# A two-layer recurrent network on one core: three gating products moved from GpSimd to VectorE

## The reference

```python
xc = silu(conv(x_in)); p = xc @ W_x
delta = softplus(p[..., :D_STATE] @ W_dt + b_dt)
h = h * d_t[:, None, :] + B_t[:, :, None] * x_t[:, None, :]   # scan over t
ys = h.sum(axis=1) * C_t
y = ys * silu(res); s = y @ W_out
...
gate = zeros_like(probs).at[arange, topk_i].add(topk_p)        # top 4 of 16
act = gelu(xt @ routed_up) * gate
g = shared + act @ routed_down
x = x + s * silu(g)
```

## Time and profile before

| | |
|---|---|
| median of 3 runs | 760.62 us (760.37 to 761.76) |
| the profiled execution | 760.88 us |
| its span, first to last instruction | 759.1 us |
| busy: TensorE / VectorE / ScalarE / GpSimd | 649.5 / 671.9 / 506.1 / 339.0 us |
| mean granted TensorE clock | 0.975 of full speed |

### The profile page before, as it was taken

One profiled execution on the slowest core, in us unless ns is written; L12 is line 12 of the kernel. 1 busy time (PEld: TensorE's weight loads), 2 busy tenths in 40 slices (PEclk: granted clock), 3 DMA queues, 4 the chain that ended last, 5 costly groups with the idle time before them and its releaser, 6 DMA issues. The chain is left out here.

```text
span 759.1 us, 10868 instructions
## 1 busy us (share of the span) xinstructions
PE 649.5 (86%) x2711; PEld 300.9 (40%) x2711; DVE 671.9 (89%) x1435; ACT 506.1 (67%) x800; POOL 339.0 (45%) x310
## 2 busy tenths in 40 slices
PE   3795999999999975679989989988988988998985
PEld 1342444444444433234434434433433433443432
DVE  4996999999999997498999899898999999999885
ACT  2472566666766653786776777678678678677774
POOL 6446567776777640134224323423423423432341
PEclk9898999999999998799999999999999999999998
DMA  6430000000000000000000000000000000000000
GB/s 156 109 85 14 0 0 0 0 0 0 0 0 0 1 0 1 0 2 0 15 14 1 14 14 0 15 14 0 14 14 14 0 14 14 0 14 14 0 15 28
DMA packets 10740, 11.29 MB, mean 15 GB/s; under 512 B 4800, under 2 KB 6288, under 8 KB 10720
## 3 DMA queue, kind: packets, MB, share of 16 engines
q1 hardware_dynamic: 9744, 10.73, 4.9%
q0 software_dynamic: 112, 0.33, 0.2%
q10 hardware_dynamic: 864, 0.00, 0.1%
HBM read 6.87 MB, written 4.19 MB: 15 GB/s over the span
## 5 line engine op out<-in xcount | busy, mean ns | idle before, releaser
L1057 PE MATMUL bank<-arena,w 128*128 128x512 f16 x640 | 153.9, 389 | 20.2 <-DVE arena L723 14.1
L1057 PE MATMUL bank<-arena,dnT 128*128 128x512 f32 x288 | 145.1, 604 | 23.4 <-DVE arena L944 23.4
L618 ACT ACTIVATE arena<-bank,xinv 128x512 f32<-128x512 f32 x144 | 95.0, 687 | 58.9 <-PE bank L1057 58.8
L1057 PEld LDWEIGHTS bank<-arena,w 128*128 128x128 f16 x640 | 63.4, 100 | 99.2 <-issue 24.6
L441 POOL TENSOR_TENSOR arena<-arena 128x512 f32<-128x512 f32 x48 | 61.1, 1303 | 59.9 <-ACT arena L555 59.9
L451 POOL TENSOR_TENSOR arena<-arena 128x512 f32<-128x512 f32 x32 | 50.1, 1565 | 84.3 <-DVE arena L985 73.8
L431 POOL TENSOR_TENSOR arena<-arena 128x512 f32<-128x512 f32 x16 | 17.5, 1092 | 150.1 <-DVE arena L923 150.1
L1057 PE MATMUL bank<-xh,upH 128*128 128x512 f16 x144 | 55.9, 388 | 29.3 <-ACT arena L618 26.5
L481 ACT ACTIVATE arena<-bank 128x512 f16<-128x512 f32 x96 | 53.9, 606 | 35.0 <-PE bank L1057 35.0
L1057 PEld LDWEIGHTS bank<-arena,dnT 128*128 128x128 f32 x288 | 51.1, 190 | 62.9 <-DVE arena L944 46.4
L944 DVE TENSOR_TENSOR arena<-arena 128x512 f32<-128x512 f32 x80 | 75.8, 965 | 0.0
(11 more groups left out here) (188 smaller groups left out, 1480.2 us busy)
## 6 DMA issues: line engine op xcount, KB each, us to landing
x_all<-in_L_attn_x SPq DMA_DIRECT2D x16, 256.0 KB, 2.7
out<-x_all SPq DMA_DIRECT2D x16, 256.0 KB, 2.0
up_n<-in_L_ffn_routed_up SPq DMA_DIRECT2D x1, 512.0 KB, 3.9
dn_n<-in_L_ffn_routed_down SPq DMA_DIRECT2D x1, 512.0 KB, 5.4
wx<-in_L_attn_W_x SPq DMA_DIRECT2D x1, 288.0 KB, 2.8
k_u<-in_L_ffn_k POOLq DMA_DIRECT2D x1, 256.0 KB, 5.2
w_in<-in_L_attn_W_in SPq DMA_DIRECT2D x1, 256.0 KB, 2.5
k_u<-in_L_ffn_k SPq DMA_DIRECT2D x1, 128.0 KB, 6.0
```

The lines of the kernel that those rows point to most:

```text
L618: a.activation(act[:, c, :], q_U[c % 2][:, :], ACT.Gelu, scale=xinv[:, I_UP:I_UP + 1]).then_inc(sem["b_act"], 1)
L1057: return nc.tensor.matmul(ps, lhsT, rhs, start=start, stop=stop)
```

## The change

`GP`, the number of gating products on GpSimd, and its semaphore `b_actp` are gone. VectorE now does all eight (`RC`): `gated(5)` between the second `scan_input` and the first `softplus`, and `gated(6)` and `gated(7)` between `state(0)` and `state(1)`. The waits on the products, on ScalarE and TensorE, all name VectorE's semaphore `b_actg`.

```diff
@@ GpSimd, layer1
-                if has(m):
-                    for c in range(GV, RC):
-                        pool.wait_ge(sem["b_act"], UC * m + c + 2)
-                        after(pool, sem["b_down"], UC * m)
-                        pool.wait_ge(sem["b_gate"], m + 1)
-                        g.tensor_tensor(prod[:, c, :], act[:, c + 1, :], gate[:, :], ALU.mult).then_inc(sem["b_actp"], 1)
@@ ScalarE, gates_out
-                    after(actv, sem["b_actg"], GV * m)
-                    after(actv, sem["b_actp"], GP * m)
+                    after(actv, sem["b_actg"], RC * m)
@@ ScalarE, gelu
-                        if c > GV:
-                            actv.wait_ge(sem["b_actp"], GP * m + c - GV)
-                        elif c:
-                            actv.wait_ge(sem["b_actg"], GV * m + c)
+                        if c:
+                            actv.wait_ge(sem["b_actg"], RC * m + c)
@@ VectorE, layer1
                     scan_input(0)
                     scan_input(1)
+                    gated(5)
                     softplus(0)
                     softplus(1)
                     state(0)
+                    gated(6)
+                    gated(7)
                     state(1)
@@ TensorE, expert_out
-                    if c > GV:
-                        pe.wait_ge(sem["b_actp"], GP * m + c - GV)
-                    elif c:
-                        pe.wait_ge(sem["b_actg"], GV * m + c)
+                    if c:
+                        pe.wait_ge(sem["b_actg"], RC * m + c)
```

More of the change, by code:

```diff
@@ L34 @@
 b_mx b_lg b_pe b_sum b_rs b_top b_fill b_rep b_gt b_gx b_gtT b_gate
-b_up b_act b_actg b_actp b_down b_d b_xdt b_e b_em b_ln b_delta b_c b_cr b_z b_zh b_zl b_b b_bx b_scan b_y b_s b_g b_sg b_sgT b_out
+b_up b_act b_actg b_down b_d b_xdt b_e b_em b_ln b_delta b_c b_cr b_z b_zh b_zl b_b b_bx b_scan b_y b_s b_g b_sg b_sgT b_out
 stored
@@ L59, in build @@
     assert G % 2 == 0
-    GP = 3
-    GV = RC - GP
     I_IN, I_UP, I_RW, I_WX, I_DT, I_CW, I_CB = range(7)
```

## The result

The changed kernel takes 767.15 us (median of 5 runs, 765.08 to 768.95) against 760.62 us before (759.04 to 762.17): a ratio of 1.0074, 95% interval 1.0055 to 1.0094. It is slower, by some 6.5 us between the medians where 4.4 were forecast, and inside the range of 761 to 771. The profiled execution took 765.08 us, with a span of 763.3 us.

A forecast was written before the change was run, and what follows sets the result against it. A ring over `sg`, convolution, SiLU and `gp` bounds the kernel before; the bound passes to the ring over `yb` and `w_out`. Steady rounds 13 x 0.17 = +2.2, ends +2.25, total +4.4: 765.0 us, range 761.0 to 771.0.

The forecast's parts named there:

- the second ring: Last scan, GpSimd's second `yb` product, TensorE from `w_out` to router, row maximum on VectorE; slack 0.50 us a round.
- two rings: One over `sg`, convolution, SiLU, ScalarE with TensorE and `gp`; a close one over last scan, `yb`, `w_out`, row maximum.
- Three products at 0.60 us: VectorE between first `scan_input` and end of `state(1)`: three more gating products, +1.80 us a round.
- The lock's 1.08 us: VectorE's first gating product no longer stands behind GpSimd's three; its pitch falls from 1.68 to 0.60 us.
- The slack behind `yb`: TensorE's `w_out` starts 0.56 us behind `yb` but could follow by 0.06, leaving 0.50 us a round.
- +0.17 us a round: Sum for a steady round: +1.25 at the row maximum less 1.08 from the first gating product.
- TensorE absorbs 0.50 us: Ahead of `w_out`: of the 1.80 us by which `yb` comes later, `w_out` moves by only +1.30.
- The ends: Rounds outside the 13 steady ones: -0.4 + 1.30 - 0.45 + 1.80 = 2.25 us.
- The faster case: Rival: GpSimd's second `yb` goes first and ends some 0.5 us earlier; 757.6 us, at its limit 750.6; chance 0.12.
- the add and the power on GpSimd: Rival: the lock stays, both get in before VectorE's first product; +1.45 us a round, 781.7 us; chance 0.05.
- the third new product: VectorE between the scans: meets the first `yb` product and takes about 1.7 us, all scans staying at 0.66.

The follow-up runs named there:

- The ninth product: Changed kernel with `gated(7)` repeated once more per round: ahead of the scans 779.33 us, at the turn behind `sg` 768.53 us.
- The experiment with the lock alone: Kernel before, three products still on GpSimd, `gated(0)` moved behind the first two convolution taps: 749.41 us, ratio 0.9854.
- the best move between the engines: Kernel before with one product, `gated(5)`, moved from GpSimd to VectorE behind `scan_input`, two left on GpSimd: 749.60 us, ratio 0.9845.
- the first product at the turn: Changed kernel with `gated(0)` moved from behind the row maximum to ahead of `low_z`: 763.20 us, ratio 1.0039 to the kernel before.
- the last kernel: Kernel before with `gated(0)` behind three convolution taps and, on ScalarE, the SiLU into `gp` ahead of the gates' copy: 747.63 us, ratio 0.9840.

## Why the prediction was right, and where its sizes were off

**What bounds the kernel, and the rings.** Right. The slack of the second ring was small, and the changed kernel has TensorE waiting for `yb` in every round. The ninth product shows it directly. The prediction named two rings; the experiments found two more that take over, at 27.59 us a round in one kernel and at 26.7 in three.

**Three products at 0.60 us.** Right, by the pitch of the new rows and by the ninth product. From the row maximum to the end of the second `yb` (621.20 + 1.64 = 622.84) a round took 622.84 - 600.39 = 22.45 us before, and 596.52 - 573.36 = 23.16 now: +0.71, where 1.80 - 1.08 = 0.72 was forecast.

**The lock's 1.08 us.** Right for the product, which went from 1.75 to 0.68 us, and L413, the small add on GpSimd, gave way: it takes 0.69 us beside a product of 0.68. The experiment with the lock alone shows the product at the same length, and that a round could give back only 0.84 us of it before another ring took over.

**The slack behind `yb`.** Here the sum was too small: +0.17 us a round was forecast, +0.38 measured. The term "TensorE absorbs 0.50 us" was mis-sized, for two reasons. The 0.06 us from `yb` to `w_out` was read in the last round, which stands outside the loop; in the 12 rounds inside the loop it is 0.13 us each time, and in the 4 outside 0.05 to 0.06. (Inside the loop the value waited for comes from the loop's counter; that this is the reason is not shown.) And from `w_out` to the row maximum it is 4.63 us (568.73 to 573.36) when TensorE starts from idle, against 4.55 when it comes without a gap: the four matmuls take 1.98 us then, not 1.88. The third part was the row maximum, for which 0.05 us of slack was assumed; the 4.63 us leave none. The three parts, 0.07, 0.08 and 0.05, are the 0.2 us that were missing. Over the 13 steady rounds the row maxima moved by 5.2 us where 2.2 were forecast (349.96 to 712.94 after, 352.71 to 710.44 before).

**The ends.** -0.4 for the first round was about right (27.07 to 26.80 us, -0.3). +1.30 for the last round with new input is 1.2 measured (712.94 to 735.90 us, before 710.44 to 732.22). For the round after it I forecast 1.80 - 0.45 = 1.35; from `w_out` to `w_out` it is +1.6. From there to the end the profile after has 6.95 us and the one before 8.00, where TensorE's clock had fallen: -1.1. So the ends came to 1.4 us where 2.25 were forecast, and hid 0.8 of the 3.0 us by which the steady rounds were too low. That is luck: no term of the sum stood for the clock.

**Why the profiled execution shows +4.2 and the median +6.5.** TensorE's clock in the opening. The stretches from 300 to 320 us, before and after (the column behind POOL is the granted clock):

```profile
310.00:320.00 10.00, 7.23 (x24) 3.46 (x25) 2.99 (x18) 7.04 (x11) 1.48 (x1) 0.56 0.00 0
```

```profile
310.00:320.00 10.00, 7.94 (x33) 3.52 (x33) 2.17 (x10) 8.01 (x12) 1.48 (x1) 0.83 0.00 1
```

The first line is the kernel before, at 0.56 of full speed, the second the changed one, at 0.83. The profiled execution after reached the row maximum of the first gating round at 323.16 us, before at 325.64. Counted from there to the end of the span it is 440.1 against 433.5 us: +6.7, which agrees with the medians. By this measure the forecast of +4.4 was 2.2 us low: 3.0 by the slack in the steady rounds, less the 0.8 at the ends.

**The rivals.** The faster case rested on GpSimd's second `yb` going first; it did not, 1.63 us as before. That the add and the power on GpSimd (L415 and L417 before) would both get in ahead of the first product did not happen: it took 0.68 us. That the third new product would take 1.7 us came true in 3 of 16 rounds only (last section). The Trainium skill, "SBUF — State Buffer", section "Who interferes with whom", calls the port that VectorE and GpSimd share an exclusive lock. The lock-alone run agrees: the product takes 0.68 us when it starts behind GpSimd's three, and 1.75 when it starts beside them.

## What to carry to other kernels

Before moving work between engines, write down the rings that close a round, with the slack of each: an instruction costs its full length on the ring that bounds and nothing beside it, and the same 0.60 us product was worth +0.60 or 0.00 by its place alone. If two engines exclude each other, look first for another order of the same work: setting one instruction 1.4 us later gave 10.6 us, as much as the best move between the engines, and moving all three products spent that gain and more. Taking work off one ring pays only until the next ring bounds, as the forecasts for the first product at the turn and for the last kernel found out. Where slack is read from a round outside the loop, add what a wait inside the loop costs.

## What the runs showed of the hardware that was not expected

**Who gets the port when both engines want it.** Before, the `yb` product asked for it during the third scan and had it ahead of the fourth (1.52 us from 591.45, of which 1.04 bare). In the changed kernel it asks at 591.49, during `gated(6)`, and in 13 of 16 rounds two more VectorE instructions go ahead of it: it takes 2.72 us, and the second scan of `state(1)` has the wait, not the product `gated(7)` as I had said. In the other three rounds `gated(7)` has it and the `yb` product takes 1.58. The cost to VectorE is nearly the same in both: the two scans take 2.29 us in place of 1.26, or the two products 2.34 in place of 1.26. What decides it is not shown.

**TensorE's clock within a steady round.** In the kernel with the first product at the turn, two rounds were about 1 us longer than their neighbours. Three stretches around one of them, and two matmuls in it:

```profile
390.00:394.00 4.00, 2.04 (x10) 0.70 (x8) 3.79 (x20) 3.97 (x7) 1.04 (x1) 1.00 0.03 10
394.00:399.00 5.00, 4.75 (x14) 1.92 (x13) 5.00 (x10) 3.23 (x6) 0.48 (x1) 0.66 0.12 45
399.00:404.00 5.00, 5.00 (x24) 2.85 (x23) 5.00 (x5) 1.65 (x3) 2.73 (x2) 1.00 0.00 0
```

```profile
393.55 0.39 PE L1048 MATMUL bank<-xh,upH 128*128 128x512 f16 x1 [1.96 <-ACT arena L607]
...
396.14 0.63 PE L1048 MATMUL bank<-xh,upL 128*128 128x512 f16 x1
```

The granted clock is 0.66 on the mean of 394 to 399 us, between its levels of 2.4 and 1.2 GHz, behind an idle time of 1.96 us and a stretch at full clock; matmuls that take 0.38 us take 0.63 there. The kernel before and the changed one kept 1.00 from 350 to 700 us. Why this kernel did not is not shown.
